# Attention outputs kept transposed: normalised by DMA and GpSimd, maxima turned by VectorE, maxima ahead of scores

## The chip, the cores and the metric

The kernel runs on one core of a Trainium2 chip. A core has TensorE (PE in the profile; PEld is its weight load), VectorE (DVE), ScalarE (ACT), GpSimd (POOL) and SyncE (SP), which here only issues DMAs. Each engine runs its own instruction stream; streams meet in semaphores. The metric is the device time of one launch in microseconds (us).

## What is computed

`x` is (4, 1024, 256). An attention by sampled windows, a layer norm, a second block with attention and a mixture of experts, and a layer norm follow each other:

```python
x = _layernorm(x + _L0_attn_ref(x, ...), axis=-1)       # windows of 33 sampled rows, gate, projection
x = _layernorm(x + _L0_ffn_ref(x, ...), axis=-1)

def _msa(x, w_qkv, w_proj):                              # B, N = 4, 1024; H = 16 heads of DK = 16
    qkv = (x @ w_qkv).reshape(b, n, 3, H, DK)
    ...
    attn = softmax(einsum("bhnd,bhmd->bhnm", q, k) / sqrt(DK))
    y = einsum("bhnm,bhmd->bhnd", attn, v).transpose(0, 2, 1, 3).reshape(b, n, d)
    return y @ w_proj
x = x + _msa(_layernorm(x, ln1_w, ln1_b), w_qkv, w_proj)
x = x + _moe_mlp(_layernorm(x, ln2_w, ln2_b), ...)       # top 1 of 8 experts, by argmax of the gate
```

The expert of a token is an argmax, so the scores are kept precise: q and k are each split in two parts, and three products of parts are stacked along the contraction (48 rows), with two more rows (50) that subtract each query's maximum, itself split in two parts.

## The kernel before

The stages follow each other: window sampling, gate and q/k/v projection (`gate_and_project`), `attention`, `project_and_route`, `experts`. The change is in attention and in what it hands to the stage behind it.

**Units and steps.** Attention has 32 units, one for each batch and pair of heads, each of 8 steps. A step takes one tile of 128 keys: four score products (`scores`, S: 2 heads x 2 halves of 512 queries, L1803) go into a ring of three PSUM banks (`BANKS`), four exponentials on ScalarE (L1691) bring them to `at_p`, and a block of four matmuls (`values`, V, L1813) adds the tile's values into one bank `at_pacc`, 32 rows for each half and head: 16 rows of outputs and 16 equal rows of the denominator, from ones beside the values. V of a step comes one step later. Score k may only start when exponential k-3 is done.

**Maxima.** The query maxima of a unit are taken ahead of it, while other units run: a maximum (M, L1781) is a pair of matmuls, one for each head, into one of two slots of two banks (`SLOTS`), and VectorE reduces 128x1024 of it (L1704). Two fall in each step; the first 6 of a unit's 16 are made two units ahead, the other 10 in the unit before. The order on TensorE in a step is `ORDER = "SMSEMSSV"`, where E is an extra in the sixth and third step: in the sixth, `turn_tops` (L1788) transposes the maxima (128x16) into a slot and VectorE splits them from there in two parts of 16x128 (L1715, L1717); in the third, `turn_out` (L1795) transposes the copied accumulator in four matmuls into a slot, and VectorE inverts the denominators (L1721) and multiplies (L1727) into `at_yn`. Both take a turn in the ring of two slots. The copy of the accumulator out of PSUM is ScalarE's, after the fifth exponential of the next unit (L1685).

**DMA order.** SP alone issues the attention's DMAs, in this order per unit: 12 loads of q and k parts and one of values for the unit three ahead (`load`, L1041, L1042, L1607); every second unit half an expert's `w2` (L1637), in the others the store of two units' outputs into `Y` in two DMAs (`store_y`, L1622); then the four rows of maxima for the next unit (`store_top`, L1049), from 8 partitions of `at_top` into one partition of `at_q`; then, in eight units, a pad of 258 KB. TensorE starts a unit only when its rows of maxima have landed (`rows_in`).

**Behind attention.** `project_and_route` works on nine chunks of up to 512 tokens: it loads `Y` by tokens, TensorE transposes it (L2195), ScalarE copies it (L2031), TensorE projects (L2204), VectorE adds and routes. The first chunk's turn and projection lie in the last unit of attention (`turn_first`, `project_first`).

## Time and profile before

| | |
|---|---|
| runs, median of 3 | 1647.42 us (1637.7 to 1650.97) |
| profiled execution, its own time | 1646.13 us |
| its span | 1643.3 us |
| mean granted TensorE clock | 0.973 |
| attention, first exponential to last copy | 519.8 to 1271.3 us |

A row of a timeline gives start, length, engine, line, operation and tiles of instructions merged in time (xN: so many), and in brackets how long the engine had been idle and what ended that. A fp32 matmul is recorded as two, so V counts x8. SPq is SP's queue of DMA issues; its length is the issue, not the transfer.

### The profile page before, as it was taken

Reading aid. Unit: us, or ns where it says so; the run is one execution under the profiler, and the core shown is the slowest. Engines: PE = TensorE matmul, PEld = TensorE weight load, DVE = VectorE, ACT = ScalarE, POOL = GpSimd, SP = SyncE. Lnnn points to the kernel's source line nnn. Section 1 sums busy time; section 2 is a strip of 40 time slices with the busy share of each in tenths; the row PEclk is TensorE's granted clock in tenths of the full one; section 3 lists DMA queues with packets and bytes.
Section 4 is the critical chain, followed back from the end, with each engine's and each line's share of the span. In section 5 each row is a group of like instructions: output and inputs, shape, how many; then the busy total and the mean of one; then the engine's idle time right before and its main releaser. Section 6 shows DMA issues by size and latency. Waiting matters only on the chain. (4 is left out here: it accounts for less than half of the span.)

```text
span 1643.3 us, 28821 instructions
## 1 busy us (share of the span) xinstructions
PE 1493.4 (91%) x10138; PEld 861.5 (52%) x10138; DVE 1283.4 (78%) x2433; ACT 1007.5 (61%) x1713; POOL 199.6 (12%) x376
## 2 busy tenths in 40 slices
PE   7688998979999999999999999999998869999997
PEld 7565665656554333333333333333333738999997
DVE  6899999845666888888888888888880767777773
ACT  3699999934334777777777777777775633222221
POOL 3011111132110000000000000000000451222222
PEclk9799999999999999999999999999997979999999
DMA  3300110027957223322233222322301657566561
GB/s 109 90 8 14 50 44 21 23 88 262 292 188 200 69 65 77 78 67 59 71 72 79 59 59 72 72 51 55 75 17 52 201 210 244 209 212 212 202 201 61
DMA packets 148700, 176.25 MB, mean 107 GB/s; under 512 B 71744, under 2 KB 106560, under 8 KB 148560
## 3 DMA queue, kind: packets, MB, share of 16 engines
q1 hardware_dynamic: 143152, 160.95, 33.0%
q0 software_dynamic: 4432, 13.24, 2.0%
q8 instruction: 82, 1.34, 0.3%
q14 instruction: 58, 0.48, 0.1%
q10 hardware_dynamic: 976, 0.24, 0.1%
HBM read 120.75 MB, written 53.43 MB: 106 GB/s over the span
## 5 line engine op out<-in xcount | busy, mean ns | idle before, releaser
L1691 ACT ACTIVATE at_p<-at_pst 128x512 f32<-128x512 f32 x1024 | 539.4, 603 | 199.2 <-PE at_pst L1803 199.1
L1704 DVE TENSOR_REDUCE at_mx<-at_pmx 128x2 f32<-128x1024 f32 x490 | 583.3, 1222 | 90.0 <-PE at_pmx L1781 85.6
L1803 PE MATMUL at_pst<-at_q,at_k 50*128 50x512 f32 x1024 | 368.5, 447 | 5.8 <-ACT at_p L1691 3.5
L1781 PE MATMUL at_pmx<-at_k,at_q 48*128 48x512 f32 x980 | 267.4, 461 | 51.5 <-DVE at_mx L1704 51.5
L1803 PEld LDWEIGHTS at_pst<-at_q,at_k 50*128 50x128 f32 x1024 | 159.8, 188 | 290.7 <-ACT at_p L1691 255.1
L1813 PE MATMUL at_pacc<-at_p,at_v 128*32 128x512 f32 x2048 | 277.1, 613 | 2.1
L878 PE MATMUL ws_pA<-ident,ws_A 128*128 128x128 f32 x1088 | 151.1, 285 | 24.0 <-ACT ws_A L660 21.3
L1781 PEld LDWEIGHTS at_pmx<-at_k,at_q 48*128 48x128 f32 x980 | 117.9, 185 | 101.9 <-DVE at_mx L1704 99.0
L878 PEld LDWEIGHTS ws_pA<-ident,ws_A 128*128 128x128 f32 x1088 | 121.1, 145 | 83.7 <-ACT ws_A L660 38.9
L2362 DVE STREAM_TRANSPOSE ex_zr<-ex_row 32x64 f32<-32x64 f32 x608 | 143.1, 235 | 15.2 <-DMA ex_row<-scratch_routed 7.4
L2402 PE MATMUL ex_pH<-ex_zT,ex_w 128*128 128x128 f32 x1248 | 145.8, 275 | 2.3 <-ACT ex_zT L2339 2.3
L2402 PEld LDWEIGHTS ex_pH<-ex_zT,ex_w 128*128 128x128 f32 x1248 | 145.3, 192 | 4.5 <-issue 2.6
L2412 PE MATMUL ex_pY<-w,ex_hT 128*128 x624 | 141.0, 379 | 0.0
L2412 PEld LDWEIGHTS ex_pY<-w,ex_hT 128*128 128x128 f32 x624 | 115.7, 190 | 14.1
L2347 ACT ACTIVATE ex_hT<-ex_pH 128x1024 f32<-128x1024 f32 x39 | 39.9, 1023 | 121.8 <-PE ex_pH L2402 121.8
L660 ACT ACTIVATE ws_A<-ws_steps,par_beta,par_alpha 128x672 f32<-128x672 bf16 (+2 forms) x128 | 99.9, 855 | 2.8 <-issue 2.2
L660 ACT ACTIVATE ws_A<-lent_steps,par_beta,par_alpha 128x672 f32<-128x672 bf16 (+2 forms) x128 | 100.2, 855 | 1.7 <-issue 1.7
L782 DVE TENSOR_TENSOR ws_AT<-ws_pA,lent_hits 128x768 f32<-128x768 f32 (+2 forms) x96 | 90.8, 952 | 9.2 <-PE ws_pA L878 8.7
L782 DVE TENSOR_TENSOR ws_AT<-ws_pA,ws_hitT 128x768 f32<-128x768 f32 (+2 forms) x96 | 89.9, 953 | 9.6 <-PE ws_pA L878 9.2
L1979 POOL MEMSET pg_eps<- 128x1 f32 x1 | 0.1, 98 | 752.9 <-POOLq L1531 752.9
L1813 PEld LDWEIGHTS at_pacc<-at_p,at_v 128*32 128x32 f32 x2048 | 41.4, 108 | 74.9 <-issue 39.8
L2339 ACT ACTIVATE ex_zT<-ex_zr,pg_lnb,pg_lnw 128x128 f32<-128x128 f32 x76 | 33.4, 486 | 73.8 <-DVE ex_zr L2362 73.8
(278 smaller groups left out, 1546.6 us busy)
## 6 DMA issues: line engine op xcount, KB each, us to landing
ex_w<-in_L_ffn_w SPq DMA_DIRECT2D x39, 1024.0 KB, 5.5
at_q<-scratch_qs SPq DMA_DIRECT2D x192, 64.0 KB, 2.8
at_k<-scratch_ks SPq DMA_DIRECT2D x192, 64.0 KB, 2.9
ex_row<-scratch_routed SPq DMA_DIRECT2D x39, 258.0 KB, 5.0
scratch_qs<-gp_split SPq DMA_DIRECT2D x16, 512.0 KB, 4.1
scratch_ks<-gp_split SPq DMA_DIRECT2D x16, 512.0 KB, 3.6
scratch_v<-gp_v SPq DMA_DIRECT2D x8, 1024.0 KB, 5.5
at_v<-scratch_v SPq DMA_DIRECT2D x32, 256.0 KB, 3.6
```

What stands on the lines that cost most here:

```text
L660: nc.scalar.activation(A[:, h % QUAD, cols(g, r)], KB[g][:, cols(g, r)], ACT.Exp, bias=par["beta"][:, t, h], scale=par["alpha"][:, t, h]). ...
L782: v.tensor_tensor(AT[h // QUAD][:, home(h, m[0]):home(h, m[-1]) + 1, :].rearrange("p s l -> p (s l)"), p[:, 0:len(m) * P], mask, ALU.mult) ...
L878: last = nc.tensor.transpose(p[:, to], a, ident[:])
L1691: a.activation(pt[k // 2 % 4][:, k % 2, :], pst[bank(w, k)][:], ACT.Exp).then_inc(exped, 1)
L1704: v.reduce_max(mx[u % 2][:].rearrange("p (h n) k -> p h n k", h=2)[:, :, j // 2, j % 2], slot(w, j)[:], AX.X).then_inc(taken, 1)
L1781: last = nc.tensor.matmul(slot(w, j)[:, h, :], att.rows(qst[u], h, ROWS)[:, nt * P:(nt + 1) * P], att.rows(kst[u], h, ROWS)[:, kh * HALF:( ...
L1803: nc.tensor.matmul(pst[bank(w, k)][:], att.rows(kst[u], h, FULL)[:, t * P:(t + 1) * P], att.rows(qst[u], h, FULL)[:, p * HALF:(p + 1) * HA ...
L1813: last = nc.tensor.matmul(pacc[at:at + 2 * DK, :], vst[u][:, s, h, :], pt[(2 * s + p) % 4][:, h, :], start=(s == 0), stop=(s == BT - 1))
L2347: a.activation(hT[j % 2][:], pH[j % 2][:], ACT.Gelu_apprx_tanh).then_inc(gelu, 1)
L2362: last = v.transpose(zr[j % 2][c * Q:(c + 1) * Q, :, q * Q:(q + 1) * Q], z[q * Q:(q + 1) * Q, :, c * Q:(c + 1) * Q])
L2402: last = nc.tensor.matmul(pH[j % 2][:, c, :], w1[j % WBUFS][:, k, c * P:(c + 1) * P], zT[j % 2][:, k, :], start=(k == 0), stop=(k == KC - 1))
L2412: last = nc.tensor.matmul(pY[j % 2][:], hT[j % 2][:, c, :], w2[:, c, bass.ds(e, 1), :], start=(c == 0), stop=(c == HC - 1))
```

## The change

Per half step (16 per unit) TensorE's order becomes: a maximum, two scores, and in every second half step a block of values of both query halves. The four matmuls of the block still have 512 columns each, now one quarter of each half (`at = (2h+c)*32`); they lag by two half steps as before. Nothing else goes into the slots.

- The maxima are combined, negated and split on VectorE in 128x32 and turned there in 32x32 blocks (`Scores.tops`); each of the four rows is then stored in four pieces, so 16 DMAs per unit (`store_top`).
- The accumulator is copied after the third exponential of the next unit (`COPY`) and stays transposed. SP folds the four denominator rows into `at_den` (`fold`, 4 DMAs), VectorE inverts them after the eighth half step (`invert`), SP writes them to DRAM, waits for that to land and reads them back as broadcasts (`spread`, 1 + 4), GpSimd multiplies (`normalise`), SP stores the outputs into `YT` (`store`, 4 DMAs).
- `project_and_route` loads `YT` by channels and projects at once, without a turn and a copy, into two PSUM buffers. The last unit's outputs are normalised beside its first chunks.
- ScalarE waits for the stores of the stage before ahead of its first exponential.

```diff
+    TOPS = 3
+    TURN = 5
+    Q = 32
+    LOADS = 2 * 2 * len(STACK) * 16 + 16
+    TOP_ROWS = 2 * 2 * 4 * 16
...
+    def tops(self, dve, w):
+        u = w % 2
+        c = Chain(dve, self.split, w * self.TOPS)
+        hi, lo = (self.top2[u][:, n * self.PIECES:(n + 1) * self.PIECES] for n in range(2))
+        c.link(dve.tensor_tensor(self.top_[:], self.mx[u][:, :, 0], self.mx[u][:, :, 1], ALU.max))
+        c.link(dve.tensor_scalar(hi, self.top_[:], -1.0, None, ALU.mult))
+        c.link(dve.scalar_tensor_tensor(out=lo, in0=self.top_[:], scalar=-1.0, in1=hi.bitcast(F32), op0=ALU.mult, op1=ALU.subtract))
+        dve.transpose(self.turned[u][:], self.top2[u][:].bitcast(F32)).then_inc(self.topT, 1)
+
+    def store_top(self, eng, w):
+        eng.wait_ge(self.topT, w + 1)
         for h in range(2):
             for n in range(2):
-                at = h * self.BASE + self.ROWS + n
-                eng.dma_start(self.qst[u][at:at + 1, :].bitcast(F32).rearrange("o (t n) -> o t n", t=BT),
-                              self.top2[u % 2][h * BT:(h + 1) * BT, n, :].bitcast(F32)).then_inc(self.rows_in, 16)
+                at, c = h * self.BASE + self.ROWS + n, n * self.PIECES + h * BT
+                row = self.qst[w % self.RING][at:at + 1, :].bitcast(F32).rearrange("o (t i j) -> o t i j", t=BT, j=self.Q)
+                for i in range(P // self.Q):
+                    eng.dma_start(row[:, :, i, :], self.turned[w % 2][i * self.Q + c:i * self.Q + c + BT, :]).then_inc(self.rows_in[w % 2], 16)
...
+class Outputs:
+    PARTS = 4
+    QUARTER = L // 4
+    FOLD = 16
+    MOVES = PARTS * 16
...
+    def fold(self, sp, w):
+        rows = P // self.PARTS
+        sp.wait_ge(self.oed, w + 1)
+        for part in range(self.PARTS):
+            at = part * 2 * DK + DK
+            sp.dma_start(self.den[w % 2][part * rows:(part + 1) * rows, :],
+                         self.oe[w % 2][at:at + 1, :].rearrange("o (a b) -> o a b", b=self.FOLD)).then_inc(self.den_in, 16)
+
+    def invert(self, dve, w):
+        dve.wait_ge(self.den_in, (w + 1) * self.MOVES)
+        dve.reciprocal(self.inv[w % 2][:], self.den[w % 2][:]).then_inc(self.inverted, 1)
+
+    def spread(self, sp, w):
+        sp.wait_ge(self.inverted, w + 1)
+        sp.dma_start(self.rden[w, :].rearrange("(a b) -> a b", b=self.FOLD), self.inv[w % 2][:]).then_inc(self.inv_out, 16)
+        sp.wait_ge(self.yd, w)
+        sp.wait_ge(self.inv_out, (w + 1) * 16)
+        for part in range(self.PARTS):
+            at, n = part * 2 * DK, L // 2
+            sp.dma_start(self.rd[at:at + DK, :],
+                         self.rden[w:w + 1, part * n:(part + 1) * n].to_broadcast([DK, n])).then_inc(self.rd_in, 16)
+
+    def normalise(self, pool, w):
+        pool.wait_ge(self.rd_in, (w + 1) * self.MOVES)
+        pool.tensor_tensor(self.oe[w % 2][:], self.oe[w % 2][:], self.rd[:], ALU.mult).then_inc(self.yd, 1)
+
+    def store(self, sp, w):
+        b, pair = w // (H // 2), w % (H // 2)
+        sp.wait_ge(self.yd, w + 1)
+        for h in range(2):
+            rows = self.yT[...].rearrange("d (p c j) -> d p c j", p=2, c=2)
+            for c in range(2):
+                at = (2 * h + c) * 2 * DK
+                sp.dma_start(rows[:, :, c, :], self.oe[w % 2][at:at + DK, :].rearrange("d (p j) -> d p j", p=2)).then_inc(self.y_out[w % 2], 16)
...
@@ attention, SP @@
+            def unit(w):
+                if w:
+                    outputs.fold(sp, w - 1)
+                    if w + 3 < UNITS:
+                        sp.wait_ge(pv, w * STEPS)
+                        load(w + 3)
+                if w % 2:
+                    load_w2(w)
+                elif 0 < w <= 2 * E:
+                    pad(w // 2 - 1)
+                if w:
+                    outputs.spread(sp, w - 1)
+                if w + 1 < UNITS:
+                    att.store_top(sp, w + 1)
+                if w:
+                    outputs.store(sp, w - 1)
+                if w == UNITS - 2:
+                    load_first()
@@ attention, ScalarE @@
+            for w in range(UNITS):
+                for k in range(2 * STEPS):
+                    n = w * STEPS + k // 2
+                    if k % 2 == 0 and n >= BUFS:
+                        a.wait_ge(pv, n - BUFS + 1)
+                    a.wait_ge(scored, w * 2 * STEPS + k + 1)
+                    a.activation(pt[:, n % BUFS, k % 2, :], pst[(w * 2 * STEPS + k) % BANKS][:], ACT.Exp).then_inc(exped, 1)
+                    if k == COPY and w:
+                        out(w - 1)
@@ attention, TensorE @@
+            for w in range(UNITS):
+                pe.wait_ge(att.rows_in[w % 2], (w // 2 + 1) * att.TOP_ROWS)
+                for s in range(STEPS):
+                    n = w * STEPS + s
+                    m = beside(w, s)
+                    if m:
+                        maxima(*m)
+                    for h in range(2):
+                        scores(n, h)
+                    if n >= LAG:
+                        values(n - LAG)
+                    if w == UNITS - 1 and s >= PROJECTED and s % 2 == 0 and (s - PROJECTED) // 2 < first.T:
+                        project_first((s - PROJECTED) // 2)
...
@@ project_and_route, TensorE @@
-            def turn(i):
...
+            def project(i):
+                pe.wait_ge(y_in[i % 2], (i // 2 + 1) * 16)
+                if i >= 2:
+                    pe.wait_ge(added, i - 1)
                 for t in range(SIZES[i]):
                     for k in range(KC):
-                        last = nc.tensor.matmul(pO[:, t, :], yT[:, k, t * P:(t + 1) * P], wp[:, k, :],
+                        last = nc.tensor.matmul(pO[i % 2][:, t, :], yT[i % 2][:, k, t * P:(t + 1) * P], wp[:, k, :],
                                                 start=(k == 0), stop=(k == KC - 1))
```

`LAG` and `COPY` are 2, `INVERT` is 7, `STEPS` 16, `BANKS` 3, `BUFS` 4.

## Rows read from the trace of the kernel before

**Rows 1.** The page: busy time of the engines, share of the span, instructions.

```profile
PE 1493.4 (91%) x10138; PEld 861.5 (52%) x10138; DVE 1283.4 (78%) x2433; ACT 1007.5 (61%) x1713; POOL 199.6 (12%) x376
```

**Rows 2.** Windows: 27 units of attention (start:end, length, busy per engine, PEclk, DMA).

```profile
569.40:1196.66 627.26, 577.66 (x3594) 211.14 (x3591) 546.83 (x568) 465.02 (x893) 0.00 (x0) 1.00 0.28 68
```

**Rows 3.** Timeline, ScalarE: two copies of the accumulator (start, length, engine, line, tiles).

```profile
1196.66 0.58 ACT L1685 COPY at_oe<-at_pacc 128x512 f32<-128x512 f32 x1
1219.87 0.58 ACT L1685 COPY at_oe<-at_pacc 128x512 f32<-128x512 f32 x1
```

**Rows 4.** Timeline: one step of attention, from its first score to the next step's.

```profile
1004.59 0.50 PE L1803 MATMUL at_pst<-at_q,at_k 50*128 50x512 f32 x1
1005.13 2.06 ACT L1691 ACTIVATE at_p<-at_pst 128x512 f32<-128x512 f32 x4 [0.54 <-PE at_pst L1803]
1005.17 0.50 PE L1781 MATMUL at_pmx<-at_k,at_q 48*128 48x512 f32 x2
1005.37 2.36 DVE L1704 TENSOR_REDUCE at_mx<-at_pmx 128x2 f32<-128x1024 f32 x2 [0.25 <-PE at_pmx L1781]
1005.51 0.77 PE L1803 MATMUL at_pst<-at_q,at_k 50*128 50x512 f32 x2
1005.78 0.18 PEld L1803 LDWEIGHTS at_pst<-at_q,at_k 50*128 50x128 f32 x1 [0.31 <-ACT at_p L1691]
1006.21 1.06 PE L1813 MATMUL at_pacc<-at_p,at_v 128*32 128x512 f32 x8
1007.21 0.50 PE L1803 MATMUL at_pst<-at_q,at_k 50*128 50x512 f32 x1
```

**Rows 5.** Timeline: values of two steps without maxima, in the last unit.

```profile
1260.95 1.06 PE L1813 MATMUL at_pacc<-at_p,at_v 128*32 128x512 f32 x8
1263.56 1.07 PE L1813 MATMUL at_pacc<-at_p,at_v 128*32 128x512 f32 x8
```

**Rows 6.** Timeline, TensorE: maxima behind the turned outputs and behind the turned maxima.

```profile
991.38 0.50 PE L1781 MATMUL at_pmx<-at_k,at_q 48*128 48x512 f32 x2 [0.73 <-DVE at_mx L1704]
1000.32 0.50 PE L1781 MATMUL at_pmx<-at_k,at_q 48*128 48x512 f32 x2 [0.99 <-DVE at_mx L1704]
```

**Rows 7.** Timeline, SP's queue: loads, a long issue, values' load, four maxima rows.

```profile
569.33 0.42 SPq L1041 DMA_DIRECT2D at_q<-scratch_qs  x1
572.12 0.42 SPq L1041 DMA_DIRECT2D at_q<-scratch_qs  x1
572.58 1.90 SPq L1042 DMA_DIRECT2D at_k<-scratch_ks  x1
993.02 0.42 SPq L1607 DMA_DIRECT2D at_v<-scratch_v  x1
1000.79 2.69 SPq L1049 DMA_DIRECT2D at_q<-at_top  x4
```

**Rows 8.** The DMA view: KB each, median us from issue to landing.

```profile
w<-in_L_ffn_w SPq DMA_DIRECT2D x16, 512.0 KB, 4.6
lent_xe<-in_L_attn_x SPq DMA_DIRECT2D x32, 10.0 KB, 2.0
scratch_v<-gp_v SPq DMA_DIRECT2D x8, 1024.0 KB, 5.5
```

**Rows 9.** Timeline, SP's queue: a short issue of the experts' stage.

```profile
1361.74 0.34 SPq L2289 DMA_DIRECT2D ex_row<-scratch_routed  x1
```

**Rows 10.** Windows and timeline, TensorE: the first three steps of attention.

```profile
519.30:528.40 9.10, 9.08 (x40) 4.03 (x40) 6.28 (x6) 6.30 (x12) 0.67 (x2) 0.62 1.06 179
519.32 0.46 PE L1803 MATMUL at_pst<-at_q,at_k 50*128 50x512 f32 x1 [2.31 <-PEq L1133]
```

**Rows 11.** Lines by form, in the window of rows 2: a small operation of VectorE.

```profile
L1709 DVE TENSOR_TENSOR at_top<-at_mx 128x16 f32<-128x16 f32 x27 | 4.7, 175 | 0.9
```

**Rows 12.** Lines by form, GpSimd: a product of 128x1024.

```profile
L311 POOL TENSOR_TENSOR ws_A<-ws_A,ident 128x1024 f32<-128x1024 f32 x1 | 2.4, 2353 | 0.1
```

**Rows 13.** Timeline, SP's queue: the last store before attention.

```profile
517.00 0.36 SPq L1154 DMA_DIRECT2D scratch_v<-gp_v  x1
```

More of the change, by code:

```diff
@@ L1594, in _, with beside, nth, load @@
+        def beside(w, s):
+            ahead, j = (1, EARLY + s) if s < TURN else (2, s - TURN)
+            return (w + ahead, j) if w + ahead < UNITS else None
+        def nth(w, j):
+            return (w - 1) * STEPS + j - EARLY
         @block.sync
         def _(sp):
-            def place(i, u):
-                per = H // 2 // RING
-                return i // per, (i % per) * RING + u
-            def load(i, u):
-                b, pair = place(i, u)
+            def load(w):
+                b, pair, u = w // (H // 2), w % (H // 2), w % RING
@@ L1648, in _ @@
+            load(2)
+            load(3)
             for dst, src in later:
@@ L1730, in unit @@
-            def unit(w, i, u):
-                for s in range(BT):
-                    ms = beside(w, u, s)
-                    for n in range(PER):
-                        if n == 1 and extra(w, s) == "out":
-                            invert(w - 1)
-                            normalise(w - 1, i if u else i - 1, (u - 1) % RING)
-                        if n == 1 and extra(w, s) == "top":
-                            split_tops(w + 1, u + 1)
-                        if ms:
-                            maximum(*ms[n])
-                    if s == TURN - 1 and turns(w):
-                        tops(w + 1, u + 1)
@@ L1744, in _, with maximum @@
-            units(unit)
-            dve.wait_ge(later_in, 16 * len(later))
-            dve.wait_ge(first.turned, 1)
-            for k in range(KC):
-                ins = v.tensor_copy(yT[:, k, :], pY[k])
-            ins.then_inc(first.yTd, 1)
-            invert(UNITS - 1)
-            normalise(UNITS - 1, UNITS // RING - 1, RING - 1)
+            def maximum(w, j):
+                n = nth(w, j)
+                dve.wait_ge(paired, n + 1)
+                v.reduce_max(mx[w % 2][:].rearrange("p (h n) k -> p h n k", h=2)[:, :, j // 2, j % 2], pmx[n % SLOTS][:], AX.X).then_inc(taken, 1)
@@ L1752, in _ @@
+            for w in range(UNITS):
+                for s in range(STEPS):
+                    m = beside(w, s)
+                    if m:
+                        maximum(*m)
+                    if s == INVERT and w:
+                        outputs.invert(v, w - 1)
+                    if s == TURN - 1 and m:
+                        dve.wait_ge(taken, nth(*m) + 1)
+                        att.tops(v, w + 1)
             dve.wait_ge(first.outed, 1)
@@ new lines, in values @@
+            def values(n):
+                w, s = n // STEPS, n % STEPS
+                u, t, p = w % RING, s // 2, s % 2
+                if p == 0:
+                    return
+                first = 0
+                pe.wait_ge(exped, 2 * n + 2)
+                if s == 1 and w:
+                    pe.wait_ge(oed, w)
+                for h in range(2):
+                    for c in range(2):
+                        at = (2 * h + c) * 2 * DK
+                        out = pacc[at:at + 2 * DK, first * QUARTER:(p + 1) * QUARTER].rearrange("d (p j) -> d p j", j=QUARTER)
+                        last = nc.tensor.matmul(out, vst[u][:, t, h, :], pt[:, n % BUFS - p + first:n % BUFS + 1, h, c * QUARTER:(c + 1) * QUARTER],
+                                                start=(s == 1), stop=(s == STEPS - 1))
+                last.then_inc(pv, 2)
@@ L1876, in projection_weights @@
+            for n in range(UNITS * STEPS - LAG, UNITS * STEPS):
+                values(n)
 def projection_weights(sb, io):
@@ L1949, in _ @@
             for i in range(1, CHUNKS):
[L1950 to L1953 removed]
+                if i == LAST_UNIT - 1:
+                    outputs.spread(sp, UNITS - 1)
+                if i == LAST_UNIT:
+                    outputs.store(sp, UNITS - 1)
                 if i >= 2:
[L1955 to L1956 removed]
+                    outputs.stored(sp, FIRST[i] // BT)
+                    sp.wait_ge(outed, i - 1)
+                    first.load(sp, dr["YT"], i, FIRST[i], SIZES[i])
                     sp.wait_ge(summed, i - 1)
@@ L2249, in _ @@
                     gate(pp)
-                if i is not None and i + 1 < CHUNKS:
-                    turn(i + 1)
                 if prev is not None:
```

388 lines of the change are left out of this document (102 added, 286 removed).

## The prediction

> **What bounds the kernel now.** I read the page first: TensorE is busy 91% of the span, VectorE 78% [rows 1]. Attention is 32 units of 8 steps. Two copies of the accumulator, one per unit, lie 23.21 us apart [rows 3], and over 27 units the clock is full and TensorE busy 92% [rows 2]. But ends of matmuls are modelled, so I went on to the timeline of one step, where the reader is to see which wait closes the loop [rows 4].
>
> The step is 2.62 us (1004.59 to 1007.21). The first score product starts at 0; its exponential starts at 0.54 and takes 0.60, to 1.14; only then is its bank free for the fourth score product, whose weight load starts at 1.19 after a wait for ScalarE; the values' block starts at 1.62, the next step at 2.62. The third bank closes the loop, not VectorE: its two maxima need 2.36, and steps that have no maxima at all take the same 2.61 from values to values [rows 5]. Eight steps are 20.9, so 2.3 of the unit's 23.2 is extra: TensorE stands 0.73 for the slot after the turned outputs and 0.99 for the one after the turned maxima [rows 6]; the rest is the turns themselves. SP, the only queue of this stage, issues per unit 13 loads, 4 rows of maxima, one output store and 0.75 of a w2 load or a pad: some 9.6 us of 23.2 by rows 7, idle otherwise.
>
> **The change, part by part.**
> 1. *Turns gone from TensorE.* Five turns and the slots that they hold leave each unit: at most the 2.3 above.
> 2. *Maxima first in the half step* (M SS M SSV in place of S M S M S S V). A pair of maxima matmuls now stands between the values and the first scores. In rows 4 the scores behind such a pair start 0.34 after it (1005.17 to 1005.51). A score that doesn't come first has no exposed weight load and is ready about 0.39 after its start (0.50 less 0.11, estimate from these rows), its exponential 0.04 later: 0.77 instead of 0.54. The whole chain moves by 0.23, the step is 2.85, eight are 22.8: +1.8 per unit. VectorE's 2.36 stays beneath it.
> 3. *Copy after the unit's third exponential instead of the fifth.* It must wait for the old unit's last values, which run from 1.85 to 2.91 (1.06 in rows 4); copy 2.95 to 3.53, so the fourth exponential is at about 3.4, and the second step ends 0.3 later.
> Parts 1 to 3 together: 22.8 + 0.3 = 23.1 against 23.2, nothing. These two costs hide behind part 7 where that is longer.
> 4. *Values in quarters of both halves.* Four matmuls per step on four column groups as before, in one block: 0.
> 5. *VectorE.* Four operations of 16 to 32 columns (nearest row 0.175 [rows 11]), with their waits 1.0 after the tenth maximum, and a reciprocal; they replace operations of about the same sum. A step leaves VectorE 2.85 - 2.36 = 0.49, so this is caught up in two steps: 0; were that cover gone, 1 per unit.
> 6. *GpSimd* multiplies 128x512 per unit; 128x1024 took 2.35 [rows 12], so about 1.2, beside everything, and only SP's last stores wait for it: 0.
> 7. *SP's queue, the part that decides.* Per unit it now issues 4 (denominators, out of one partition into 32), 13 loads, 1 (inverses to DRAM), 4 (back, broadcast), 16 (maxima rows, four pieces for each of four), 4 stores, and w2 or a pad: 42.75 for 18.75. Loads follow each other by 0.465 (569.33 to 572.12, six of them [rows 7]). A maxima row, from 8 partitions of SBUF into one, takes 2.69 / 4 = 0.67. A piece is again 8 partitions into 8 runs, only shorter, and the issue doesn't go by bytes (the 256 KB load of values has the same 0.42 as the 64 KB ones), so I take 0.67; the least is 0.34, the shortest issue that I found [rows 9]; 0.465 is the case between.
>
> The order in SP's queue, counted from the unit's first instruction on TensorE: the copy has ended, 3.6; 4 x 0.465, 5.5; 13 loads and 0.4 for the occasional long issue (one took 1.90), 11.9; w2 or pad, on average 12.3; the reciprocal, after the eighth half step, is out at 12.0. Then a new wait, for the inverses to land: 2.0 (a 10 KB load [rows 8]), 14.3; behind a w2 load, itself 4.6 to landing, it may be up to 2.6 later, of which I take half in every second unit: 15.0. Queued behind that wait are the broadcasts, to 16.8, and the maxima rows. The maxima themselves are ready at 4 x 2.85 + 0.3 + 2.9 (second reduction of the fifth step) + 1.0 = 15.6. The last of 16 pieces starts at 16.8 + 15 x 0.67 = 26.9 and lands at 28.9. TensorE needs these rows before the next unit's first instruction and would have been there at 23.1: it stands 5.8 in every unit, and ScalarE and VectorE with it. The stores lie behind the pieces, in time in which SP waits anyway. The queue's own sum, 26.75 x 0.465 + 10.7 = 23.1, is already a unit long. Units 29 and 30 have no loads: pieces from 15.9, rows landed at 28.0. Unit 0, with neither values in its first step nor a copy: 26.4.
> 8. *The clock.* A stand of 2.31 ahead of attention was followed by the low level (1.2 GHz; mean 0.62 over 9.1 us [rows 10]): three steps, up to the start of the fourth, took 9.1 where 1.62 (no values in the first) + 2.62 + 2.62 = 6.9 are due: 2.2 lost. After each stand of 5.8 I expect one such fall, part of it inside the stand: 1.2 per unit, with 0 and 2.2 as its ends. The Trainium skill ("TensorE: Matmul & The Clock Gate", HAM oscillation) describes blocks of matmuls between DMA waits that start cold every time; no run shown here has such a periodic stand.
> 9. *Ends.* ScalarE now waits for the last store of the stage before (issued 517.0, 5.5 to landing, 522.5) with its first exponential, now at 519.9 (519.32 + 0.54): +2.7 [rows 10, 13]. In the projection a turn and a ScalarE copy leave each of eight chunks, mostly beside VectorE's work; less the new wait for the last unit's denominators I take -3 (ends 0 and -8). The last unit loses eight turns: -2.
>
> **The sum.** Units 1 to 28: (28.9 + 1.2 - 23.2) x 28 = 193. Units 29 and 30: (28.0 + 1.2 - 23.2) x 2 = 12. Unit 0: 26.4 + 2.2 for its fall, against 20.0 + 2.2 + 1.0 now: 5.4. Ends: -2.3. Together +208 on this execution's 1646.1 (span 1643.3 and 2.8 around it; the runs' median 1647.4 is 0.1% above it): 1854.
>
> **The rivals.**
> *B, pieces at a load's price.* No long issue, w2 effect or fall: pieces from 15.9, the last at 22.9, landed 24.9: +1.7 x 28 = 48, and 3 for the rest: 1697. For it: a piece carries a quarter of a row's bytes. Against: bytes don't show in the issue times.
> *C, no change.* SP in time, only parts 1 to 3 and the ends, -2.3: 1644. It decides below (23.1 - 15.6 - 2.0) / 15 = 0.37 per piece.
> *C by a page.* A sentence of the Trainium skill ("DMA: Bandwidth & Descriptors", Issuing engines are not separate DMA queues) says that the time to initiate a DMA on the sequencer is "usually small relative to the DMA itself". With SP's issues free this becomes case C. Rows 7 and 8 speak against it: 0.42 and 0.67 to issue beside 2.0 to landing, one after the other.
> *D, faster.* SP in time, and the fourth score not held by its bank, so that part 2 costs nothing: unit 8 x 2.61 + 0.3 = 21.2, -2.0 x 31 = -62: 1584. It decides at (21.2 - 14.6 - 2.0) / 15 = 0.31 per piece, with the maxima ready at 14.6; no issue in the rows is that short.
> *E, worse.* Every unit pays the full fall and the full landing behind w2: +1.65 x 28: 1900; with 0.67 for the 8 denominator and output moves too, 1.6 more each: 1945.
>
> **Chances.** Forecast with its own spread (1790 to 1890) 0.60, E 0.11, B 0.14, C 0.06, D 0.09. A measurement of this kernel tells about 1% from nothing. Faster by over 1%: 0.09; within it: 0.06; slower: 0.85. The range takes in B and most of E: 1690 to 1925.
>
> **What would show it.** SP issuing without a break behind the copy, the pieces at 0.67 last in each unit; TensorE standing 5 to 6 at each unit's start until the maxima rows land; the low clock after it; copies 29 to 31 apart; steps of 2.85 at full clock. Wrong would be: pieces under 0.4; steps of 2.61 (part 2); or a unit of 29 whose wait lies elsewhere, as values waiting for the copy or a maximum for VectorE.

## The result: 21.6% slower, and where the time went

| | before | after |
|---|---|---|
| median of 4 runs | 1642.56 us (1633.8 to 1650.97) | 1997.08 us (1984.04 to 2007.48) |
| ratio | | 1.216, 95% interval 1.205 to 1.226 |
| profiled execution, its span | 1646.13, 1643.3 | 2002.27, 2000.2 |
| mean granted TensorE clock | 0.973 | 0.774 |
| attention, first exponential to the start of the last copy | 519.8 to 1271.3 | 524.8 to 1630.3 |

The direction and the mechanism came as forecast (SP's queue, its pieces last, TensorE standing for them, the low clock); the time is 143 us above the forecast of 1854 and 72 above the end of the range. Here and below a median is over all executions, and a ratio leaves out those that took over 1.5% longer than the fastest of their kernel.

The page of the kernel after, its busy times, the clock in 40 slices, and the lines that answer to those of before (columns as in rows 1; the two lines behind PEclk are the chain of work that ended last, by engine and by line):

```profile
PE 1805.6 (90%) x9914; PEld 973.4 (49%) x9914; DVE 1271.0 (64%) x2431; ACT 999.6 (50%) x1705; POOL 238.9 (12%) x409
...
PEclk8899999999855555587868756755655579899999
...
PE 54%; SPq 10%; DMA 4%; DVE 2%; issue 2%; ACT 1%; POOL 1%; POOLq 0%; ACTq 0%; DVEq 0%
PE at_pacc L1758 16%; PE at_pst L1742 13%; PE at_pmx L1733 10%; SPq L1130 7%; PE ex_pH L2303 7%; PE ex_pY L2313 7%; DMA scratch_rden<-at_inv 2%; DMA at_q<-at_topT 1%; DVE at_mx L1706 1%; SPq L1058 1%; SPq L1109 1%; SPq L1110 1%; PE pg_pO L2107 1%; POOL scratch_routed L1932 1%; ACT at_p L1694 0%
...
L1742 PE MATMUL at_pst<-at_q,at_k 50*128 50x512 f32 x1024 | 444.6, 596 | 24.1 <-ACT at_p L1694 23.7
...
L1733 PE MATMUL at_pmx<-at_k,at_q 48*128 48x512 f32 x980 | 313.5, 636 | 76.4 <-DMA at_q<-at_topT 74.0
...
L1064 POOL TENSOR_TENSOR at_oe<-at_oe,at_rd 128x512 f32<-128x512 f32 x32 | 40.8, 1275 | 1059.9 <-DMA at_rd<-scratch_rden 1059.9
```

TensorE's busy time has grown by 312 us [rows 1] for fewer instructions: nearly the same matmuls, many of them at the low clock. A 5 of PEclk is half of full speed; the 5s fill half of attention. The chain has SP's issues in it, 10% of the span, 7 of them the pieces (L1130): the new bound in part of the units. TensorE's idle time ahead of the maxima, 76.4, is nearly all for `at_topT`: 14 stands of 2.2 to 8.2, 5.3 in the mean. (A stand is such a wait of TensorE at a unit's start for its rows of maxima.)

The windows of the kernel after, over three long stretches and a mixed one (columns as in rows 2):

```profile
546.50:846.00 299.50, 295.37 (x1045) 106.41 (x1049) 161.09 (x172) 140.11 (x270) 10.20 (x8) 0.51 0.21 47
846.00:1020.00 174.00, 133.65 (x672) 51.04 (x672) 102.82 (x110) 90.19 (x175) 6.39 (x5) 0.80 0.23 53
...
1142.00:1235.00 93.00, 92.83 (x328) 33.51 (x324) 51.49 (x53) 44.23 (x85) 2.53 (x2) 0.50 0.22 48
1422.00:1614.00 192.00, 189.97 (x660) 66.40 (x656) 95.03 (x100) 91.74 (x176) 6.35 (x5) 0.50 0.17 42
```

Rows 2 showed a clock of 1.00 throughout. Now there are stretches at 0.50 (1.2 GHz) of some 294, 93 and 192 us, and a fourth, not shown, of some 96 from 1315. TensorE is busy 99 to 100% in them and doesn't stand; each begins behind a stand (4.13 in the first window, which is why that reads 0.51). The window from 846 is mixed: a clock of 0.80, TensorE 77% busy, a stand in each unit. The copies of the accumulator tell the same: of the 31 distances from one to the next 15 are 36.4 us, all of them at the low clock, 15 lie between 31.3 and 35.5 (mean 33.6), the last one is 23.6. Before, 29 of them were 23.2 [rows 3], and the last two 24.9 and 26.5.

The chain of waits through one mixed unit, from the landing of its rows to that of the next unit's (start, length, what):

```profile
1006.79 1.65 DMA at_q<-at_topT
...
1008.49 0.80 PE at_pmx L1733 x2
...
1011.25 1.86 PE at_pacc L1758 x8
1013.12 0.72 PE at_pmx L1733 x2
...
1024.91 1.86 PE at_pacc L1758 x8
1026.78 0.74 PE at_pmx L1733 x2
...
1027.54 2.37 DVE at_mx L1706 x2
...
1030.80 0.71 SPq L1130
...
1040.33 0.62 SPq L1130
1041.00 1.65 DMA at_q<-at_topT
```

The reader is to see four links: four steps of TensorE and the maxima of a fifth, here all at the low clock (4.55 a step), then VectorE's last maxima at 1027.54, then sixteen issues of SP without a gap (10.8), then the landing, 1.65 from the last issue's start. What SP does before them (start, length, queue, line, tiles, count):

```profile
1013.79 2.47 SPq L1042 DMA_DIRECT2D at_den<-at_oe  x4
1016.31 1.47 SPq L1109 DMA_DIRECT2D at_q<-scratch_qs  x1
...
1023.38 0.58 SPq L1621 DMA_DIRECT2D scratch_routed<-at_padrow  x1
1025.53 0.33 SPq L1053 DMA_DIRECT2D scratch_rden<-at_inv  x1
1028.29 1.71 SPq L1058 DMA_DIRECT2D at_rd<-scratch_rden  x4
1030.80 10.83 SPq L1130 DMA_DIRECT2D at_q<-at_topT  x16
1041.68 1.83 SPq L1074 DMA_DIRECT2D scratch_YT<-at_oe  x4
```

The four moves of the denominators take 0.62 each, the broadcasts 0.43, a piece 0.68. Between 1025.86 and 1028.29 SP waits for the inverses, issued at 1025.53, to land: 2.76 from the issue. In five of the six units that I followed (842 to 1043) the pieces start right behind the broadcasts, 20.7 to 21.7 after the unit's first matmul; in the sixth, this one, with the maxima, 22.3 after it.

TensorE's timeline at either level, the stand ahead of this unit and one step at the low clock, one step at the full one:

```profile
1008.49 0.80 PE L1733 MATMUL at_pmx<-at_k,at_q 48*128 48x512 f32 x2 [6.69 <-DMA at_q<-at_topT]
...
1013.04 0.79 PE L1733 MATMUL at_pmx<-at_k,at_q 48*128 48x512 f32 x2
...
1034.65 0.50 PE L1733 MATMUL at_pmx<-at_k,at_q 48*128 48x512 f32 x2
...
1036.13 0.50 PE L1742 MATMUL at_pst<-at_q,at_k 50*128 50x512 f32 x1 [0.28 <-ACT at_p L1694]
...
1037.56 0.50 PE L1733 MATMUL at_pmx<-at_k,at_q 48*128 48x512 f32 x2
```

The stand is 6.69 (the one at this unit's own end is only 2.16, since the low clock has stretched the unit beside SP's work); the step is 4.55 (1008.49 to 1013.04) at the low clock and 2.91 (1034.65 to 1037.56) at the full one, where the fourth score waits 0.28 for its bank, as part 2 had it.

### The profile page after: what moved, and what is told of

Same layout as the page of the kernel before. It is cut to its first block, busy times and chain, and to the rows that moved or that the text cites. A ratio compares the mean times of both kernels' runs of the same rounds, so it can differ in the third digit from the quotient of the medians.

```text
span 2000.2 us, 28586 instructions
## 1 busy us (share of the span) xinstructions
PE 1805.6 (90%) x9914; PEld 973.4 (49%) x9914; DVE 1271.0 (64%) x2431; ACT 999.6 (50%) x1705; POOL 238.9 (12%) x409
## 4 chain that ended last, share of the span: by engine, by line
PE 54%; SPq 10%; DMA 4%; DVE 2%; issue 2%; ACT 1%; POOL 1%; POOLq 0%; ACTq 0%; DVEq 0%
PE at_pacc L1758 16%; PE at_pst L1742 13%; PE at_pmx L1733 10%; SPq L1130 7%; PE ex_pH L2303 7%; PE ex_pY L2313 7%; DMA scratch_rden<-at_inv 2%; DMA at_q<-at_topT 1%; DVE at_mx L1706 1%; SPq L1058 1%; SPq L1109 1%; SPq L1110 1%; PE pg_pO L2107 1%; POOL scratch_routed L1932 1%; ACT at_p L1694 0%
## 5 line engine op out<-in xcount | busy, mean ns | idle before, releaser
L1706 DVE TENSOR_REDUCE at_mx<-at_pmx 128x2 f32<-128x1024 f32 x490 | 577.0, 1220 | 455.8 <-PE at_pmx L1733 455.8
L1694 ACT ACTIVATE at_p<-at_pst 128x512 f32<-128x512 f32 x1024 | 534.0, 599 | 504.0 <-PE at_pst L1742 498.1
L1742 PE MATMUL at_pst<-at_q,at_k 50*128 50x512 f32 x1024 | 444.6, 596 | 24.1 <-ACT at_p L1694 23.7
L1758 PE MATMUL at_pacc<-at_p,at_v 128*32 128x512 f32 x2048 | 421.3, 909 | 0.0
L1733 PE MATMUL at_pmx<-at_k,at_q 48*128 48x512 f32 x980 | 313.5, 636 | 76.4 <-DMA at_q<-at_topT 74.0
L1733 PEld LDWEIGHTS at_pmx<-at_k,at_q 48*128 48x128 f32 x980 | 135.0, 273 | 438.3 <-issue 294.6
L1742 PEld LDWEIGHTS at_pst<-at_q,at_k 50*128 50x128 f32 x1024 | 210.4, 278 | 204.6 <-ACT at_p L1694 175.7
L878 PE MATMUL ws_pA<-ident,ws_A 128*128 128x128 f32 x1088 | 149.8, 285 | 25.5 <-ACT ws_A L660 24.7
L1064 POOL TENSOR_TENSOR at_oe<-at_oe,at_rd 128x512 f32<-128x512 f32 x32 | 40.8, 1275 | 1059.9 <-DMA at_rd<-scratch_rden 1059.9
L1758 PEld LDWEIGHTS at_pacc<-at_p,at_v 128*32 128x32 f32 x2048 | 47.6, 129 | 96.3 <-ACT at_p L1694 94.9
```

Source lines behind the costliest of these rows:

```text
L878: last = nc.tensor.transpose(p[:, to], a, ident[:])
L1694: a.activation(pt[:, n % BUFS, k % 2, :], pst[(w * 2 * STEPS + k) % BANKS][:], ACT.Exp).then_inc(exped, 1)
L1706: v.reduce_max(mx[w % 2][:].rearrange("p (h n) k -> p h n k", h=2)[:, :, j // 2, j % 2], pmx[n % SLOTS][:], AX.X).then_inc(taken, 1)
L1733: last = nc.tensor.matmul(pmx[n % SLOTS][:, h, :], att.rows(qst[u], h, ROWS)[:, nt * P:(nt + 1) * P], att.rows(kst[u], h, ROWS)[:, kh * HA ...
L1742: nc.tensor.matmul(pst[k % BANKS][:], att.rows(kst[u], h, FULL)[:, t * P:(t + 1) * P], att.rows(qst[u], h, FULL)[:, p * HALF:(p + 1) * HAL ...
L1758: last = nc.tensor.matmul(out, vst[u][:, t, h, :], pt[:, n % BUFS - p + first:n % BUFS + 1, h, c * QUARTER:(c + 1) * QUARTER], start=(s == ...
```

## The experiments

Each kernel but e4 is the changed kernel with the edit shown. A length of a stretch of low clock is read from windows of 3 us with a mean under 0.6, in the one execution of each kernel that has a profile. Times are medians; the ratio is to the kernel before on the same chip. The chips differ from group to group: the kernel before took 1636.8 on that of e1 to e4, 1642.6 on that of e5 to e8 and beside the result above, 1637.0 for e9 to e12, 1640.9 for e13 and e14.

### e1: the scores first

```diff
-                    if m:
-                        maxima(*m)
-                    for h in range(2):
-                        scores(n, h)
+                    if m and s % 2:
+                        maxima(*m)
+                    scores(n, 0)
+                    if m and s % 2 == 0:
+                        maxima(*m)
+                    scores(n, 1)
```

> The changed kernel with one thing undone: the order on TensorE in a step is again S M S / M S S V in place of M S S / M S S V. Theory A (the stands of TensorE for the maxima rows bring the clock down; the place of the maxima costs only its 0.23 to 0.3 per step at full clock): the stands are still there (pieces at 0.68 after maxima ready about 14.6 into the unit, rows landed about 26.7 where the unit's work ends at 21.2), the clock still falls again and again, the mean granted clock stays under 0.85, steps at full clock are 2.61; 1880 to 1980 us. Theory B (the new order itself lets the clock fall and keeps it low): the clock is full nearly everywhere, units are 27 to 28 us, 1780 to 1800 us.

**Measured:** 1914.77, ratio 1.172 (1.169 to 1.176). Units of 30.6 to 33.2 (the last three 24.4 to 28.9), a stand of 9.19 ahead of the unit at 1006, steps of 2.67 at full clock, no stretch of low clock over 24 us. The time is theory A's and B is out, though the mean clock is 0.867 to 0.887 where A has under 0.85. The order alone is worth 82 us here (76 if each kernel is counted from the one before on its own chip): what goes with it are the long stretches.

### e2 and e3: no stand at all

The pieces are replaced by one store of the turned maxima to DRAM and four rows back; the denominators' DMAs are issued by GpSimd. e3 has e1's order as well.

```diff
+        eng.dma_start(self.dram[w, :].rearrange("(p j) -> p j", p=P), self.turned[w % 2][:]).then_inc(self.tops_out, 16)
+        eng.wait_ge(self.tops_out, (w + 1) * 16)
...
-                for i in range(P // self.Q):
-                    eng.dma_start(row[:, :, i, :], self.turned[w % 2][...]).then_inc(self.rows_in[w % 2], 16)
+                eng.dma_start(row, back[:, c:c + BT, :, :]).then_inc(self.rows_in[w % 2], 16)
@@ GpSimd @@
             for w in range(UNITS - 1):
+                outputs.fold(g, w)
+                outputs.spread(g, w)
                 outputs.normalise(g, w)
```

> The changed kernel, maxima still first, but TensorE's stand taken away: the turned maxima go to DRAM in one DMA and come back as four rows (5 DMAs for 16), and the denominators' DMAs are issued by GpSimd. Theory A: no stands, so the clock stays full; steps 2.91, units 23.6; 1650 to 1665 us, no different from the kernel before. Theory B: no stands, yet the clock is low for long stretches, units up to 36.4; above 1850 us.

> As the experiment with rows by DRAM, and the scores first in the step (S M S / M S S V). Both theories: no stands, clock full, steps 2.61, units 8 x 2.61 + 0.3 = 21.2 if the rows land in time (ready 14.6, DRAM 2.0, four issues, 2.0: 20.6 to 21): about 1585 to 1600 us, faster than the kernel before. The rival that the third bank isn't what closes the step: no difference to the experiment with maxima first.

**Measured:** e2 1654.67, ratio 1.013 (1.010 to 1.015), units of 23.5, clock 0.977; e3 1595.34, ratio 0.976 (0.974 to 0.979), units of 21.9. Both as theory A has it, so B is out again. Windows over the attention of e2, then of e3:

```profile
520.00:1270.00 750.00, 676.41 (x4043) 258.38 (x4044) 601.98 (x646) 542.21 (x1051) 181.71 (x313) 1.00 0.30 72
```

```profile
520.00:1220.00 700.00, 678.77 (x4049) 243.72 (x4053) 598.35 (x646) 546.62 (x1054) 181.98 (x313) 1.00 0.32 77
```

Without stands the clock is full in both orders. With the rows and the denominators off SP the loss is gone but for 1.3%; the order with the maxima first costs 59 us (2.90 against 2.66 per step).

### e4: the kernel before, with stands

Twelve small idle transfers ahead of the rows of maxima in each unit of the kernel before.

```diff
                 sp.wait_ge(split, w * TOPS + TOPS)
...
+                for n in range(12):
+                    sp.dma_start(dummy[...], ident[8 * n:8 * n + BT, 0:32]).then_inc(dummied, 16)
```

> The kernel before with its old order and turns on TensorE; SP issues 12 more DMAs of 8 partitions by 32 elements (into a tile that nobody reads) ahead of each unit's four maxima rows. They should cost 12 x 0.67 = 8 us of SP's queue and make TensorE stand about 5.5 at each unit's start. Theory A: the clock falls as in the changed kernel, and units are 31 to 36, 1900 to 2000 us, mean clock under 0.85. Theory B (the low clock needs the new order): stands of 5.5 and short falls of the clock, units 29 to 30, 1830 to 1860 us. If the queue isn't the cause of the stands at all: no difference to the kernel before.

**Measured:** 1876.65, ratio 1.148 (1.143 to 1.153). Stands of 5.5 to 5.9 (7.2 the first), units of 30.4 to 31.2 up to the last two, mean clock 0.903 to 0.914, many stretches of low clock and the longest under 40 us. The time lies between theory A's range and theory B's, the clock and the short falls are B's. Nothing else of the change is in it: the stands alone bring most of the loss and a low clock with it, but no long stretches. A unit costs 30.7 in the mean, and 30.7 less 23.2 and 5.55 leaves 2.0 for the clock.

### e5: the pieces away, the denominators left in SP's queue

e1 with the rows by DRAM of e2.

> The changed kernel with the scores first and the 16 pieces replaced by one store of the turned maxima to DRAM and four rows back; the denominators' moves stay in SP's queue. Theory A (SP's queue adds up to a stand, and pieces and denominators both count): the row issues end about 24.4 us after the copy's unit begins and land near 25.9, against 21.4 that TensorE needs, so a stand of about 4 in every unit, 1 to 2 for the clock, units of 27 to 28: 1740 to 1790. Rival R (the pieces alone make the stand, the denominators' moves are covered): units of 22 and 1600 to 1620. Rival L (any stand brings the low clock for hundreds of us): over 1850.

**Measured:** 1710.88, ratio 1.042 (1.038 to 1.045); units of 22 to 27, 25.5 in the mean. Below the expected 1740 to 1790, since the stands are shorter: 21 of them, 3.7 at most and 2.4 in the mean, where 4 was expected in every unit; ten units have none. From e1 to e5 it is 204 us for 11 issues fewer (11 x 0.68 x 30 = 224), from e5 to e3 116 us for the denominators' nine (210 and 110 if each is counted from the kernel before on its own chip; the clock is in these sums too, from 0.87 over 0.92 to 0.98). R and L are out: both count.

### e6 and e7: three stands in 32 units

e2 (maxima first) and e3 (scores first), with e4's twelve transfers ahead of the rows of units 6, 14 and 22 only.

> The kernel without any stand and with the maxima first (rows by DRAM, denominators' moves with GpSimd, 1655), in which 12 small idle transfers stand ahead of the rows of maxima in three units only (6, 14, 22), each making TensorE stand 6 to 7 us. Theory P (a stand tips the clock, and an unbroken stream of the order with maxima first then keeps the low level for long): after each stand a stretch of low clock of 50 us or more, 1750 or more in all. Theory Q (the low level goes by itself within 10 to 25 us, and lasts only where stands repeat in every unit): each stand costs its 6 to 7 and 3 to 8 for the clock: 1680 to 1700, longest stretch of low clock under 30 us.

> The same three stands in the kernel with the scores first (1595 without them). Both theories: 3 times 6 to 7 for the stand and 2 to 6 for the clock, 1620 to 1640, longest stretch of low clock under 30 us; if the low clock lasts here too for 50 us or more after one stand, the order has no part in it.

**Measured:** e6 1732.44, ratio 1.055 (1.051 to 1.059); e7 1638.23, ratio 0.996 (0.991 to 1.001). Windows of e6 before its stands and behind the third:

```profile
546.00:651.00 105.00, 94.88 (x571) 36.13 (x573) 87.21 (x92) 76.34 (x149) 25.57 (x44) 1.00 0.29 73
1066.00:1192.00 126.00, 125.57 (x440) 45.58 (x440) 68.03 (x71) 59.60 (x115) 19.52 (x34) 0.50 0.24 51
1195.00:1240.00 45.00, 40.90 (x245) 15.56 (x241) 37.41 (x40) 32.46 (x64) 11.09 (x19) 0.99 0.26 56
```

and of e7 behind its first, second and third stand (7.02, 6.93 and 7.05 long):

```profile
662.00:669.00 7.00, 6.65 (x37) 2.22 (x40) 4.98 (x6) 4.99 (x10) 2.04 (x4) 0.88 0.27 60
843.00:864.00 21.00, 20.94 (x87) 8.71 (x87) 12.44 (x14) 11.82 (x23) 4.55 (x9) 0.56 0.27 73
1027.00:1048.00 21.00, 16.99 (x66) 6.79 (x68) 9.59 (x9) 9.15 (x17) 2.37 (x5) 0.50 0.28 58
```

The timeline of TensorE at the first of them, where a score of 0.79 is one at the low clock and one of 0.50 at the full one:

```profile
659.85 0.79 PE L1754 MATMUL at_pst<-at_q,at_k 50*128 50x512 f32 x1 [7.02 <-DMA at_q<-scratch_tops]
...
663.87 0.50 PE L1754 MATMUL at_pst<-at_q,at_k 50*128 50x512 f32 x1
```

e6's three stands are 5.75, 5.74 and 5.74 long. In e6 the units behind them are 23.7, then 27.0, then three of 36.4 and one of 29.0: 132 us of low clock with no stand in it and no cause that the trace shows for its end. In e7 they are 21.9, 26.4, 26.4. The unit with the stand is itself longer than the stand explains, by 1.7 in e6 (31.0 against 23.5 and 5.75) and by 1.5 in e7 (30.3 against 21.9 and 7.0). So each stand brought the low clock, and beyond its own length it cost 1.4 to 1.9 twice, 5.2 to 6.1 three times, and once, with the maxima first, 46 (1.7 + 3 x 12.9 + 5.4).

e7 came as expected. e6's 1732 lies between the two theories' ranges: P's long stretch came behind one stand in three, and Q, which has none over 30 us, is out. Three of e6's four executions agree within 2 us; the fourth took 1868.69 at a mean clock of 0.816 (0.920 to 0.922 in the others) and has no profile. With three stands in each kernel, e6 and e7 alone don't prove that the order decides.

### e8: the denominators by GpSimd alone

e2's edit on GpSimd, the pieces kept.

> The changed kernel, maxima first and with its 16 pieces, but with the denominators' nine moves issued by GpSimd. SP's pieces start when the maxima are ready, 15.8 to 16.3 after the unit's start at full clock, end 27.0 and land at 28.1: a stand of 4.6 in every unit instead of 6.7. Theory P (maxima first keeps the clock low once it has fallen): long stretches of low clock as in the changed kernel, units of 32 to 34 on average, 1900 to 1970. Theory Q (the length of the stand decides): units of 29 to 30, 1820 to 1860, longest stretch under 60 us. If the pieces' start is not moved at all, the denominators did not delay them and the time is that of the changed kernel.

**Measured:** 2002.78 (1973.02 to 2026.29), ratio 1.209 (1.200 to 1.218): no gain, though in its mixed units it does what it should. TensorE there:

```profile
869.13 0.80 PE L1731 MATMUL at_pmx<-at_k,at_q 48*128 48x512 f32 x2 [4.03 <-DMA at_q<-at_topT]
```

and the window over its long stretch:

```profile
553.00:817.00 264.00, 264.00 (x930) 94.69 (x928) 142.90 (x152) 125.13 (x240) 42.91 (x74) 0.50 0.19 49
```

The stand is 4.03 where the kernel after has 5.3 in the mean, and eleven units are 29.3 to 31.1. But fourteen are 36.4, which wait for no DMA. So Q is out, and the time is above P's range (1900 to 1970) too: P holds for the long stretches, and was priced too low.

### e9 and e10: the heads of the maxima swapped

```diff
-                for h in (1, 0):
+                for h in (0, 1):
```

> The changed kernel as it is, but each pair of maxima matmuls takes head 0 ahead of head 1, so that a matmul on the upper rows (scores of head 0) no longer follows one on the same rows. Step at full clock 2.9, as before (the bank closes it). Theory U (the clock stays low because at the low level the order with maxima first leaves TensorE a step of 4.55 against 4.13 with the scores first, and no more room): the step at the low clock falls to about 4.1, no stretch of low clock over 60 us, units of 32 as with the scores first: 1900 to 1940. Theory V (the pairing of rows has no part in it): long stretches as before, 1980 to 2010, or some 10 less if only the low step is shorter.

> The kernel with three stands and the maxima first (1732, one of its stands followed by 132 us of low clock), with the heads of the maxima's pairs swapped. U: each stand costs 7.5 and 3 to 4 for the clock, 1685 to 1695, longest stretch under 30 us. V: one or more stretches of 50 us or more, 1710 or more.

**Measured:** e9 2001.12, ratio 1.221 (1.216 to 1.227), a stretch of 432 us among its low ones (that execution took 2020.49, the others 1990 to 2011); e10 1679.82 and 1682.10, 1718.72 and 1722.13, so that its median of 1700.41 means little; its profile, of the fastest, has no long stretch, and the slower two fit one long stretch each, which no profile shows. In both the step at the low clock stayed at 4.55, so they missed what they aimed at: e9 came out as theory V has it, but says nothing on U.

### e11 and e12: towards the fastest version

```diff
-    COPY = 2
+    COPY = 4
```

e11 is e3 with this; e12 also takes head 0 first where a pair of maxima follows a score of head 1.

> The fastest so far (rows by DRAM, denominators' moves by GpSimd, scores first, 1595, units of 21.9), with the accumulator copied after the next unit's fifth exponential instead of the third. The second step of a unit, now 3.2 long, goes to 2.66: 0.5 less in each of 31 units, 1575 to 1583. If the copy did not cause the long second step: 1592 to 1598.

> The same, and where a pair of maxima follows a score of head 1, head 0 comes first. If the fourth score is held by its bank, nothing moves: within 0.3% of the kernel with the copy after the fifth exponential. If TensorE's own order closes the loop, steps of 2.55 to 2.6: 10 to 15 us less.

**Measured:** e11 1588.85, ratio 0.972 (0.969 to 0.975); e12 1588.11, ratio 0.972 (0.969 to 0.975). Values around a unit's start, in e3 and in e11:

```profile
1002.50 1.06 PE L1760 MATMUL at_pacc<-at_p,at_v 128*32 128x512 f32 x8
...
1005.69 1.06 PE L1760 MATMUL at_pacc<-at_p,at_v 128*32 128x512 f32 x8
```

```profile
1016.36 1.06 PE L1760 MATMUL at_pacc<-at_p,at_v 128*32 128x512 f32 x8
...
1019.16 1.06 PE L1760 MATMUL at_pacc<-at_p,at_v 128*32 128x512 f32 x8
```

The step across the copy is 3.19 in e3 and 2.80 in e11, units 21.9 and 21.5: 0.4 in each, less than the 0.5 expected, and 12 in the span of the profiled executions. The median, 1588.85, misses both ranges, 1575 to 1583 and, had the copy no part in it, 1592 to 1598. The intervals of the two ratios overlap at their ends, so the runs alone leave e11's gain over e3 open. e12 adds nothing, as expected if the bank closes the step.

### e13 and e14: two orders between

e13 is M SS, S M S, V; e14 is S M S, S M S, V.

```diff
-                    if m:
+                    if m and s % 2 == 0:       # e14: no such line
                         maxima(*m)
-                    for h in range(2):
-                        scores(n, h)
+                    scores(n, 0)
+                    if m and s % 2:            # e14: if m
+                        maxima(*m)
+                    scores(n, 1)
```

> The changed kernel with the order M SS, S M S, V: the maxima right behind the values' block only. At the low clock one pairing of head 0 with maxima less is lost than in the changed kernel: a step between 4.13 and 4.55. Theory O (what counts is that the maxima stand right behind the values' block): long stretches as in the changed kernel, over 60 us, 1960 to 2010. Theory L (the length of the low step, TensorE at the low clock being busy without a gap in 4.55 where the step at full clock takes 2.91): no stretch over 60 us if the low step is 4.3 or less, 1900 to 1940.

> The changed kernel with S M S in both half steps, values behind the second. O: no maxima behind the values' block, so no stretch over 60 us: units of 32 to 33, 1900 to 1940. L: the same if the low step is 4.3 or less, but long stretches and 1960 to 2010 if it is 4.5 or more.

**Measured:** e13 1998.61, ratio 1.216 (1.212 to 1.220), with stretches of 336 and 237 us (an execution of 2022.82; the other four took 1987 to 1999, at mean clocks of 0.783 to 0.814); e14 1919.41, ratio 1.170 (1.167 to 1.173), none over 24 us (mean clocks of 0.852 to 0.870). Both times are theory O's. The same 260 us of each, e13 and then e14:

```profile
560.00:820.00 260.00, 259.56 (x920) 92.25 (x912) 146.04 (x150) 123.51 (x237) 8.92 (x7) 0.50 0.21 48
```

```profile
560.00:820.00 260.00, 203.39 (x1022) 80.00 (x1020) 156.03 (x168) 135.10 (x262) 10.25 (x8) 0.75 0.23 54
```

e13 differs from e14 only in the first half step, where it has the changed kernel's, and behaves as the changed kernel. So, in kernels that stand in every unit, the long stretches go with the maxima right behind the values' block: 79 us on one chip. The low step is 4.55 in e13 too, against my expectation, and 4.13 or 4.35 in e14. There a score and a maximum start together behind the values, which the pair of maxima does not do with what follows it:

```profile
590.62 0.79 PE L1742 MATMUL at_pst<-at_q,at_k 50*128 50x512 f32 x1
590.63 1.22 PE L1733 MATMUL at_pmx<-at_k,at_q 48*128 48x512 f32 x2
...
594.97 0.79 PE L1742 MATMUL at_pst<-at_q,at_k 50*128 50x512 f32 x1
```

Order and length of the low step change together in every kernel here (4.55 with the maxima first, 4.1 to 4.4 with the scores first), so theories O and L are not told apart.

## Why the prediction was wrong

**Parts 1 to 3, the step: right.** 2.91 against 2.85, bank wait and all. e2 has units of 23.5 for the 23.1 of the sum; e3 shows that the order with the scores first would have kept 1.3 of what the turns leave. The copy's 0.3 is 0.3 in e2 (23.5 less 8 x 2.90) and 0.6 in e3.

**Parts 4 to 6: right.** GpSimd's product takes 1.28 and VectorE is 64% busy; neither shows in a wait of the followed units.

**Part 7, SP's queue: right in kind, 2.1 per mixed unit short.** The order of the queue, the pieces at 0.67 (0.68), their end as the last link and the stand (5.8 forecast, 5.3 in the mean, from 2.2 to 8.2) came out. Short were the denominators' moves, 0.62 instead of 0.465 (+0.6), the loads with their long issue and the w2 or pad (+0.8), and (+0.9) the landing of the inverses: 2.8 to 4.5 and 3.6 in the mean of the six units followed, where I had 2.65 in the mean. Right behind a w2 load it took 4.46 and 4.24, right behind a pad 3.55 and 3.48, and 2.88 and 2.76 where the store was issued 2.1 us after such a transfer. That is the effect that I had only half counted; e1 shows it too, 4.24 behind a w2 load:

```profile
1020.22 0.58 SPq L1616 DMA_DIRECT2D w<-in_L_ffn_w  x1
1020.85 0.50 SPq L1053 DMA_DIRECT2D scratch_rden<-at_inv  x1
1025.09 1.71 SPq L1058 DMA_DIRECT2D at_rd<-scratch_rden  x4
1026.84 10.82 SPq L1130 DMA_DIRECT2D at_q<-at_topT  x16
```

The pieces start at 20.7 to 21.7, not at 16.8: some 19.1 by these terms, the rest by the clock, since the copy ends 5.3 after the unit's start, not 3.6. Pieces and landing together are 11.9 against 12.1, which gives 0.2 back.

**Part 8, the clock, is the step that failed.** "After each stand of 5.8 I expect one such fall, part of it inside the stand: 1.2 per unit, with 0 and 2.2 as its ends." It was sized on one fall behind one stand of 2.31 in the kernel before [rows 10], whose order has the scores first. The 148 us between this forecast and the profiled execution divide so, nearly (the ends of attention are small beside them): fifteen units at 36.4 instead of 30.1, 94 us; fifteen mixed ones at 33.6 instead of 30.1, 53, of which 2.1 x 15 = 32 are part 7's and 21 the clock's. In the mixed units the low clock comes where it is dearest, in the first steps, which hold back the copy, the eighth half step's reciprocal and the maxima, so it delays the pieces in full. The units of 36.4 I had not thought of at all: eight steps of 4.55, in which SP is in time (the pieces start at 22.3 and take 11.9, so the rows have landed 34.2 after the unit's start), so that there is no stand left to blame. Behind a single stand e6 shows them too. With the scores first the price was about right: 2.0 per unit in e4, inside my ends of 0 and 2.2, and e1, the same queue with the scores first, shows some 32 per unit and 1915 without the long stretches, inside my range. What I took without a reason was that in the new order a fall costs no more than in the old one. Even with the scores first a single one can cost 6 (e7), nearly three times my upper end.

The Trainium skill ("TensorE: Matmul & The Clock Gate", HAM oscillation) has blocks between DMA waits start cold every time. Behind the six stands of e6 and e7 the traces agree: each first matmul found a clock of 0.50, e7's first score with its 0.79 too. What differs is how long the low clock goes on from there: 4 us behind e7's first stand, 18 to 19 behind its others, 130 behind e6's last.

**Part 9, the ends.** The start cost 5.0, not 2.7 (the first exponential, at 524.78, waits for the store of `scratch_v`). Behind attention, from the start of the last copy, 369.9 instead of 372.0: -2.1 for the -3, in spite of a wait of 3.73 for the last unit's `YT`:

```profile
524.78 1.57 ACT L1694 ACTIVATE at_p<-at_pst 128x512 f32<-128x512 f32 x3 [3.20 <-DMA scratch_v<-gp_v]
...
1644.35 5.32 PE L2107 MATMUL pg_pO<-pg_wproj,first_yT 128*128 128x256 f32 x16 [3.73 <-DMA first_yT<-scratch_YT]
```

**The rivals.** B and C fall with the pieces' 0.68. "C by a page", for which SP's issues had to be as good as free, falls with e5: 11 issues fewer are 204 us. E is the nearest, but its two causes, the full fall and landing and 0.67 for all moves, give 1945 at most. D's 1584 is nearly met by e3 and e11, by another way than D's: the scores come first, so that part 2 doesn't arise, and SP's load is gone; the change then gains 2.4 to 2.8%.

**What stays open.** Why the low clock lasts with the maxima behind the values, and what ends such a stretch. A kernel that changes the length of the low step without the order wasn't found (e9 was meant to be one). The order may not be the only way to a lasting low clock either: one of seven executions of the kernel before, on the chip of e1 to e4, took 2081.82 at a mean clock of 0.638, with no stands added and the scores first. With the two levels 0.5 and 1.0 that is some 1500 us at the low one (an estimate from that mean); it has no profile, and its cause is unknown. So the order is shown to decide in the profiled kernels with stands, and not to be needed for a low clock that lasts.

## What to carry to other kernels

Count a queue in issues, not in bytes, with a row for each kind, and put the chain "wait for a landing, then more issues" in series; where it ends last, a few small DMAs more per round cost a stand in every round. A stand on TensorE is not priced by its length: the low clock behind it may outlast it by far, and how long depends on the order in the step, so take that price from runs with single stands in the order that the new kernel has (several, since e6's three differed), or keep the range open upwards by all rounds at half clock (here 8 x 4.55 = 36.4 per unit, which would have given 1646 + 31 x 13.2 = 2055 as an end). And an order that costs nothing beside a stand (2.91 for 2.66) is paid once the stand is mended.

## What the runs showed of the hardware that I had not expected

- A granted clock of 0.50 over windows of 126 us (e6, behind a single stand of 5.7) to 380 us (e9) in an unbroken stream of matmuls, TensorE 99 to 100% busy; in no profile over 40 us with a score right behind the values.
- Equal stands with unequal outcomes: in e7 behind 7 us of standing the clock was full again 4 us after the first matmul, or after 18 to 19; in e6 behind 5.7 after 6, 15 or 130.
- A fall of the clock needs no stand: in the last two units of the kernel before, of e6 and of e7, where VectorE has no maxima left, it was 0.50 for 15 to 21 us with no wait of TensorE over 0.8 in the 20 us ahead of it.
- An issue out of one partition into 32 takes 0.62, out of 8 into one 0.68, a load 0.42: so in these three it goes by the shape, not by the bytes.
- In the changed kernel a small store took 4.2 to 4.5 to land right behind a load of 512 KB on the same queue, 3.5 right behind a store of 258 KB, and 1.5 in the unit at 1141, which has neither.
